# Second attention of a two-layer block: four score banks in turn, one bank and one exponential per head, values in two visits

## The chip, the cores and the metric

One core of a Trainium2 chip. The metric is the device time of one execution in microseconds (us). The engines are PE (TensorE, matmuls, with its weight loads apart as PEld), DVE (VectorE), ACT (ScalarE), POOL (GpSimd) and SP (SyncE, which issues DMAs). Each works through its own queue in order, and they meet at semaphores.

## The reference, cut to what matters

The kernel computes two layers on 4 x 512 tokens of width 256; each adds an attention and a mixture of experts to its input. The change lies in the attention of the second layer: 32 heads of dimension 8 in 8 groups, where the four heads of a group share keys and values.

```python
q = q.reshape(Bx, Sx, N_GROUPS, R, HEAD_DIM).transpose(0, 2, 3, 1, 4)
sim = jnp.einsum('bgrsd,bgtd->bgrst', q, k) / math.sqrt(HEAD_DIM)
attn = jax.nn.softmax(sim, axis=-1)
out = jnp.einsum('bgrst,bgtd->bgrsd', attn, v)
```

## The kernel before

The second attention works on one batch (512 tokens) and one group of heads at a time: 4 batches x 8 groups. A group has 16 pairs of a tile of 128 tokens (t, of 4) and a head (r, of 4). It is computed twice. First, `scores` (L814) makes the scores of 128 queries against 512 keys in one matmul (S0 to S15 below), and DVE's `reduce_max` (L1709) takes the maximum of each query. The maxima are negated and split into two parts (L1721, L1723), transposed by PE (`maxima_t`, L851; M below) and added to the stacked queries, into `qm` (L1702). Then `scores_t` (L820) computes the scores again, transposed (128 keys against 512 queries, T0 to T15 below) with the maxima already subtracted, ACT takes the exponential (L1206) into `pt`, and `values` (L830) multiplies with the values, one visit per tile of keys with four matmuls, one per head, in four column strips of the array. A ones column in the values gives the sums. For each two groups, ACT copies the result out of bank 7 (`outputs`, L1186), PE transposes it (`outputs_t`, L843) and DVE divides (`normalise`, L1671).

These steps are staged by hand. `stage(b, s)` stands in PE's, ACT's and DVE's programs with the same 16 steps i: PE issues S_i of group s, and beside them the later parts of group s - 1 and s - 2. `TRANSPOSED` (L860) gives the step at which each T is issued and `VALUED` (L861) that of each values visit; a step of 16 or more falls into the next stage. Before, T's go in eight pairs of heads into two double banks (3 and 4, 5 and 6), with one exponential of 1024 columns for each pair (T0 and T1 at step 4, and so on). Values tiles 0 and 1 are visited at step 15, tile 2 at step 3 of the next stage, tile 3 at its step 9. T0 waits for `qm` (L887). `turns` (L295) places the transposes of the maxima behind S2, those of the outputs (every second stage) behind step 11, and in three stages of a batch (s = 5, 6, 7) one third of the next batch's projection at step 13 (`project`, six matmuls, L547 to L549), and the transposes of its values (`values_by_key`, L807) at step 12 of the last. `compact` takes a projection out: first ACT (L1178 for queries; L1181 and L1183 for keys and values), then DVE the low part (L1661, L1664), at step 15 of DVE's stage.

S, M, the outputs, the projections and the values transposes share a ring of three banks: `next_bank` (L304) makes each use wait for the reader of the third use before it. `pt` has three tiles, so an exponential also waits for the values visit three tiles earlier (L1205). On SP, `stack_keys` (L367) loads the keys of four groups in turn and waits for the transposed scores of the group four back; `stack_queries` (L381) waits for `qm`. In the first batch DVE also does the routing of the second layer's experts, one small operation per step of a stage (`to_mask1`, `to_slots1`, L1694 and L1698; what is left of the second runs behind the batch's last stage, L1743).

Of the kernel before, what the change touches and what calls it, by code (L numbers as in the profile page):

```python
# [7 lines left out]
P = 128  # L8
# [4 lines left out]
QT = S // P  # L13
# [16 lines left out]
NG, R, HD = 8, 4, 8  # L30
# [11 lines left out]
def program(nc, x_in, aw0_in, aw1_in, ws0_in, moe0_in, moe1_in, pad_in, const_in, bias_in, out):  # L42
# [3 lines left out]
    with ctx:  # L46
# [83 lines left out]
        psum = ctx.enter_context(nc.psum_tensor("psum", [P, 8, 512], f32))  # L130
# [58 lines left out]
        km = [tr(R, S) for _ in range(4)]  # L189
        mz = tr(QT, P)  # L190
        qm_both = place("qm", on1 + 4104, [P, 2, S], f32r)
        qm = [qm_both[:, n, :] for n in range(2)]
        kv = tf(S)
        va = tf(QT, NG * 32)
        pt = [tf(R, S), tf(R, S), place("pt2", M + 32848, [P, R, S])]
# [56 lines left out]
        b_pj, b_kv, b_hi, b_lo, b_vt, b_va = (sem(n) for n in ("b_pj", "b_kv", "b_hi", "b_lo", "b_vt", "b_va"))  # L252
        b_qd, b_kd, b_sn, b_mx = (sem(n) for n in ("b_qd", "b_kd", "b_sn", "b_mx"))
        b_m1, b_m2, b_mt, b_qm, b_st, b_ex = (sem(n) for n in ("b_m1", "b_m2", "b_mt", "b_qm", "b_st", "b_ex"))
        b_km = sem("b_km")
        b_pv, b_ot, b_ox, b_rc, b_on, b_nt = (sem(n) for n in ("b_pv", "b_ot", "b_ox", "b_rc", "b_on", "b_nt"))
# [37 lines left out]

        def turns(s, following):  # L295
            never = QT * R
            return {"maxima": 2, "outputs": 11, "values": 12 if s == NG + 1 else never,
                    "project": 13 if following and NG - 3 <= s < NG else never}

        ring, read = {}, []

        def next_bank(engine, use, reader, value):  # L304
            if len(read) >= 3:
                engine.wait_ge(*read[-3])
            ring[use] = psum[:, (len(read) + 1) % 3, :]
            read.append((reader, value))
            return ring[use]

        @block.sync
        def _(sp):
# [9 lines left out]
            for l in range(2):  # L322
                n = ROWS[l] // PAD
# [43 lines left out]
            def stack_keys(u):  # L367
                b, g = u // NG, u % NG
                if g == 0:
                    sp.wait_ge(b_lo, 3 * b + (2 if b else 1))  # L370
                if u:
                    sp.wait_ge(b_kd, u * R * 16)
                if u < 4:
                    sp.wait_ge(b_km, u + 3)
                else:
                    sp.wait_ge(b_st, 2 * QT * (u - 3))
                for r in range(R):
                    sp.dma_start(km[u % 4][24 * r:24 * r + 24, r, :].bitcast(f32),
                                 kc[g * HD:(g + 1) * HD].bitcast(f32)).then_inc(b_kd, 16)
# [165 lines left out]
        def _(pe):  # L545
# [249 lines left out]
            routed(0, after_attention0)  # L795
            pe.wait_ge(m_y, pairs(0, NPAIR[0]))

            NP, NQ = NG * QT * R, NG * QT

            def project(n, b1, o):  # L800

# [17 lines left out]

            def scores_t(b, g, i):  # L820

                t, h = i // 2, i % 2
                if g >= 1 or i >= 2:
                    pe.wait_ge(b_ex, b * (2 * NQ) + (g * 2 * QT + i - 1))
                for r in (2 * h, 2 * h + 1):
                    ins = nc.tensor.matmul(psum[:, 3 + 2 * h + r % 2, :], km[g % 4][:, r, t * P:(t + 1) * P],  # L826
                                           qm[g % 2], start=True, stop=True)
                ins.then_inc(b_st, 1)

            def values(b, g, t):  # L830

                pe.wait_ge(b_ex, b * (2 * NQ) + ((g * QT + t) * 2 + 2))
                n = b * NG + g
                if t == 0 and g % 2 == 0 and n:
                    pe.wait_ge(b_ot, n // 2)
                if t == 0 and g % NG == 0:
                    pe.wait_ge(b_va, b + (g // NG + 1))
                for r in range(R):
                    ins = nc.tensor.matmul(psum[32 * r:32 * r + 32, 7, :], va[:, t, g % NG * 32:g % NG * 32 + 32], pt[(n * QT + t) % 3][:, r, :],  # L839
                                           start=(t == 0 and g % 2 == 0), stop=(t == QT - 1 and g % 2 == 1), tile_position=(0, 32 * r))  # L840
                ins.then_inc(b_pv, 1)
# [15 lines left out]

            TRANSPOSED = (4, 5, 8, 11, 12, 13, 16, 17)  # L860
            VALUED = (15, 15, 19, 25)  # L861

            def follow(b, g, step):
                for n in range(2 * QT):
                    if TRANSPOSED[n] == step:
                        scores_t(b, g, n)
                for t in range(QT):
                    if VALUED[t] == step:
                        values(b, g, t)
# [127 lines left out]
        def _(act):  # L997
# [161 lines left out]
            for b in range(B):  # L1159
                for k in (2, 3):  # L1160
                    r = k * T + b * S
# [6 lines left out]
            def compact(n, b1, o, at):  # L1168

                act.wait_ge(b_pj, b1 * 3 + (at + 1))  # L1170
                if not (isinstance(b1, int) and b1 == 0):
                    if n < 2:
                        act.wait_ge(b_qd, b1 * (NG * 16) - (1 - n) * (NG // 2) * 16)
                    else:
                        act.wait_ge(b_kd, b1 * (NG * R * 16))
                if n < 2:
                    for i in range(2):
                        ins = nc.scalar.activation(qc[:, n, i, :], o, ACT.Identity, bias=bq1[:, n:n + 1])  # L1178
                    ins.then_inc(b_hi, 1)
                else:  # L1180
                    nc.scalar.activation(kv[:], o, ACT.Identity, bias=bq1[:, 2:3]).then_inc(b_kv, 1)  # L1181
                    for i in (0, 2):
                        ins = nc.scalar.activation(kc[:, i, :], o, ACT.Identity, bias=bq1[:, 2:3])  # L1183
                    ins.then_inc(b_hi, 1)
# [8 lines left out]
            def stage(b, s, last):  # L1193
                back, following = s >= 1, not last and s >= 1
                for t in range(QT):
                    if isinstance(b, int) and (b, s, t) == (0, 2, 1):
                        gating_exp(E1, 2, TT)
                    if back:
                        g = s - 1
                        for h in range(2):  # L1200
                            if s >= 2 and s % 2 and (t, h) == (1, 1):
                                outputs(b, s - 2)
                            act.wait_ge(b_st, b * (2 * NG * QT) + ((g * QT + t) * 2 + h + 1))
                            if b * (NG * QT) + g * QT + t >= 3:
                                act.wait_ge(b_pv, b * (NG * QT) + (g * QT + t - 2))  # L1205
                            nc.scalar.activation(pt[((b * NG + g) * QT + t) % 3][:, 2 * h:2 * h + 2, :], psum[:, 3 + 2 * h:5 + 2 * h, :],  # L1206
                                                 ACT.Exp, scale=float(HD) ** -0.5).then_inc(b_ex, 1)
                    if t == 2 and following and NG - 3 <= s < NG:
                        compact((0, 2, 1)[s - (NG - 3)], b + 1, ring["projection", b * 3 + s - (NG - 3) + 4], s - (NG - 3))
                if last and s == NG:  # L1210
                    outputs(b, s - 1)

# [34 lines left out]
            for n in range(2 * B):  # L1247
                act.wait_ge(b_nt, n + 1)
                b, k = n // KH, n % KH
# [627 lines left out]
```

## Time and profile before

| | us |
|---|---|
| median of 3 runs (1142.21 to 1143.25) | 1142.29 |
| the profiled execution's own time | 1137.68 |
| its span, first to last instruction | 1135.9 |
| PE busy | 1009.3 |
| DVE busy | 758.9 |
| ACT busy | 592.8 |

The profile is of one execution, which was faster than the three timed ones; its rows add up to its own span. Busy times of PE are of pipelined matmuls with modelled ends. In rows of the chain of waits a number is the time that a piece added to the chain; in rows of the timeline it is the time from the start of the first to the end of the last instruction of a merged group, so overlaps are inside. An answer names tiles by the first tensor at their place: `work_f` and `pt` are the tiles of exponentials, `work_r` holds keys, queries and the negated maxima.

### The profile page before, as it was taken

The page shows a single profiled execution, that of the slowest core. Times are in us where ns is not written, and L with a number is a line of the kernel's source. Part 1 is how long each engine was busy: PE and PEld are TensorE (multiplying, and loading weights), DVE is VectorE, ACT ScalarE, POOL GpSimd, SP SyncE. Part 2 cuts the span into 40 slices and gives each one's busy share as a digit, 9 for nine tenths or more (in the row PEclk, how much of TensorE's full clock was granted, in tenths as well). Part 3 has the DMA queues.
Part 4 walks back from the last instruction along what each step waited for, and adds up shares of the span by engine and source line. Part 5 has one row for each costly group of instructions (what it writes and reads, how often), then busy time and mean ns, then how long its engine had stood idle before and what let it go on. Part 6 is the DMA issues. An engine that isn't in the chain of part 4 may idle for free.

```text
span 1135.9 us, 17330 instructions
## 1 busy us (share of the span) xinstructions
PE 1009.3 (89%) x5716; PEld 738.8 (65%) x5716; DVE 758.9 (67%) x1575; ACT 592.8 (52%) x895; POOL 318.2 (28%) x331
## 2 busy tenths in 40 slices
PE   4999995769999846799999999999999987999995
PEld 3877874669999814555554555555555565888884
DVE  6577553466665446799888888888888846444437
ACT  6325553265565543365655666566555655444431
POOL 2005777065654510000000122222221000455442
PEclk9999998789999958899999999999999998999999
DMA  6863333364434272011111222222222124333253
GB/s 223 326 270 116 127 107 118 104 198 144 135 127 135 95 310 36 12 30 29 29 29 29 43 55 58 56 56 56 56 57 43 63 72 156 108 107 101 91 198 137
DMA packets 49139, 120.48 MB, mean 106 GB/s; under 512 B 7752, under 2 KB 24904, under 8 KB 48520
## 3 DMA queue, kind: packets, MB, share of 16 engines
q1 hardware_dynamic: 36096, 82.80, 25.2%
q0 software_dynamic: 11808, 32.37, 7.5%
q10 hardware_dynamic: 1152, 4.19, 0.9%
q8 instruction: 52, 0.85, 0.3%
q14 instruction: 31, 0.25, 0.1%
HBM read 72.30 MB, written 52.42 MB: 110 GB/s over the span
## 4 chain that ended last, share of the span: by engine, by line
PE 65%; DVE 15%; POOL 7%; ACT 5%; issue 4%; DMA 3%; SPq 0%; ACTq 0%; DVEq 0%; POOLq 0%
PE psum L817 10%; PE psum L839 10%; PE psum L826 8%; POOL xg L466 5%; PE psum L633 5%; PE psum L634 4%; PE psum L635 4%; DVE work_f L1709 4%; PE psum L547 3%; PE psum L549 3%; PE psum L548 3%; PE psum L619 3%; PE psum L644 2%; ACT work_f L1206 1%; PE psum L665 1%
## 5 line engine op out<-in xcount | busy, mean ns | idle before, releaser
L1709 DVE TENSOR_REDUCE work_f<-psum 128x1 f32<-128x512 f32 x512 | 335.0, 685 | 51.2 <-PE psum L817 49.8
L1206 ACT ACTIVATE work_f<-psum 128x1024 f32<-128x1024 f32 x172 | 169.0, 1023 | 112.0 <-PE psum L826 110.4
L817 PE MATMUL psum<-work_r 128*128 128x512 f32 x512 | 205.2, 440 | 19.5 <-DVE work_f L1709 6.5
L473 POOL DMA_INDIRECT yk<-yb,dest x134 | 131.4, 980 | 238.7 <-ACT yb L1059 215.0
L817 PEld LDWEIGHTS psum<-work_r 128*128 128x128 f32 x512 | 94.2, 190 | 131.3 <-DVE work_f L1709 75.5
L826 PE MATMUL psum<-qm,work_r 128*128 128x512 f32 x512 | 161.9, 398 | 4.2 <-ACT work_f L1206 2.7
L466 POOL DMA_INDIRECT xg<-xn,slot x112 | 108.4, 968 | 180.5 <-PE psum L855 142.8
L826 PEld LDWEIGHTS psum<-qm,work_r 128*128 128x128 f32 x512 | 93.6, 188 | 31.8 <-ACT work_f L1206 10.9
L1206 ACT ACTIVATE pt<-psum 128x1024 f32<-128x1024 f32 x84 | 82.9, 1023 | 50.2 <-PE psum L826 49.3
L633 PE MATMUL psum<-wexp,xbh 128*128 x268 | 102.5, 382 | 6.9 <-issue 6.8
L634 PE MATMUL psum<-wexp,xbh 128*128 x268 | 96.6, 360 | 0.0
L635 PE MATMUL psum<-wexp,xbl 128*128 x268 | 96.1, 359 | 0.0
L839 PE MATMUL psum<-work_f 128*32 128x512 f32 x688 | 89.1, 601 | 0.6 <-ACT work_f L1206 0.6
L1044 ACT ACTIVATE sgb<-psum 128x352 f32<-128x352 f32 (+1 forms) x67 | 34.8, 519 | 98.2 <-PE psum L635 98.2
L1482 DVE TENSOR_TENSOR xbl<-psum,xbh 128x512 fp32r<-128x512 f32 x67 | 46.3, 691 | 58.0 <-ACT xbh L999 57.6
L1059 ACT ACTIVATE yb<-psum,share 128x256 f32<-128x256 f32 x134 | 56.3, 472 | 47.8 <-PE psum L661 24.5
L462 POOL TENSOR_TENSOR xn<-const 128x16 f32<-128x16 f32 x7 | 1.5, 220 | 259.0 <-PE psum L855 185.9
L1492 DVE TENSOR_TENSOR hb<-sgb,psum 128x352 f32<-128x352 f32 (+1 forms) x67 | 39.2, 584 | 51.0 <-ACT sgb L1044 50.8
L633 PEld LDWEIGHTS psum<-wexp,xbh 128*128 128x128 f32 x268 | 52.1, 194 | 13.5 <-issue 9.7
L619 PE MATMUL psum<-const,xb 128*128 128x128 f32 x268 | 42.2, 282 | 15.3 <-DVE xbl L1482 10.1
L635 PEld LDWEIGHTS psum<-wexp,xbl 128*128 128x128 f32 x268 | 52.3, 195 | 5.0
L634 PEld LDWEIGHTS psum<-wexp,xbh 128*128 128x128 f32 x268 | 52.2, 195 | 3.8
(218 smaller groups left out, 2034.9 us busy)
## 6 DMA issues: line engine op xcount, KB each, us to landing
xb<-xg SPq DMA_DIRECT2D x67, 258.0 KB
xg<-in_pad SPq DMA_DIRECT2D x1, 10320.0 KB
yg<-yk SPq DMA_DIRECT2D x20, 512.0 KB, 9.4
stage<-in_moe SPq DMA_DIRECT2D x16, 608.0 KB, 4.8
xg<-in_pad SPq DMA_DIRECT2D x1, 7224.0 KB
work_r<-work_r SPq DMA_DIRECT2D x128, 48.0 KB
work_r<-work_r SPq DMA_DIRECT2D x32, 192.0 KB
stage<-in_moe SPq DMA_DIRECT2D x16, 384.0 KB, 3.8
```

The costliest lines, as they stand in the source:

```text
L466: nc.gpsimd.indirect_dma_start(xg[l], bass.IndirectOffsetOnAxis(ap=slot[l][:, at:at + 1], axis=0), xn[l][:, t, :], None).then_inc(m_scat, 16)
L473: nc.gpsimd.indirect_dma_start(yk[l], bass.IndirectOffsetOnAxis(ap=dest[:, j % 8, i:i + 1], axis=0), yb[l][:, j % 2, i, :], None).then_inc ...
L619: ins = nc.tensor.transpose(psum[:, 4, (i * KH + c) * P:(i * KH + c + 1) * P], xb[l][:, j % 2, i, c * P:(c + 1) * P], ident)
L633: nc.tensor.matmul(o, xbh[l][:, j % 2, i * KH + c, :], hi, start=c == 0, stop=False)
L634: nc.tensor.matmul(o, xbh[l][:, j % 2, i * KH + c, :], lo, start=False, stop=False)
L635: ins = nc.tensor.matmul(o, xbl[l][:, j % 2, i * KH + c, :], hi, start=False, stop=c == KH - 1)
L817: nc.tensor.matmul(next_bank(pe, ("scores", n), b_mx, n + 1), qs[g % 2][:, t * P:(t + 1) * P], km[g % 4][:, r, :], start=True, stop=True). ...
L826: ins = nc.tensor.matmul(psum[:, 3 + 2 * h + r % 2, :], km[g % 4][:, r, t * P:(t + 1) * P], qm[g % 2], start=True, stop=True)
L839: ins = nc.tensor.matmul(psum[32 * r:32 * r + 32, 7, :], va[:, t, g % NG * 32:g % NG * 32 + 32], pt[(n * QT + t) % 3][:, r, :], start=(t = ...
L1059: ins = nc.scalar.activation(yb[l][:, j % 2, i, :], psum[:, 6, i * H:(i + 1) * H], ACT.Identity, scale=share[:, j % 8, i:i + 1])
L1206: nc.scalar.activation(pt[((b * NG + g) * QT + t) % 3][:, 2 * h:2 * h + 2, :], psum[:, 3 + 2 * h:5 + 2 * h, :], ACT.Exp, scale=float(HD) * ...
L1709: v.reduce_max(mx[:, s % 2, i:i + 1], ring["scores", n], AX.X).then_inc(b_mx, 1)
```

## The change

PE, ACT and DVE do the same arithmetic on the same data in another arrangement.

- The ring has four banks (0 to 3) from the seventeenth use on; each use waits for the reader of the fourth use before it.
- T's go one by one, at steps 4 to 19, into three single banks (4, 5, 6) in turn. T number m waits for the exponential of number m - 3, and ACT does one exponential of 512 columns for each.
- Values tiles 0 and 1 are visited at step 14 (behind S14 and T10), tiles 2 and 3 at step 22, which is step 6 of the next stage (between S6 and T2).
- The outputs are transposed at step 12, projections and values transposes at step 10. ACT takes a projection out ahead of exponential 7, DVE at its step 12.
- `stack_keys` counts 16 matmuls per group instead of 8 pairs.

```diff
-            return {"maxima": 2, "outputs": 11, "values": 12 if s == NG + 1 else never,
-                    "project": 13 if following and NG - 3 <= s < NG else never}
+            return {"maxima": 2, "outputs": 12, "values": 10 if s == NG + 1 else never,
+                    "project": 10 if following and NG - 3 <= s < NG else never}
...
-        ring, read = {}, []
+        ring, holder, uses = {}, {3: (b_va, 1)}, []
 
         def next_bank(engine, use, reader, value):
-            if len(read) >= 3:
-                engine.wait_ge(*read[-3])
-            ring[use] = psum[:, (len(read) + 1) % 3, :]
-            read.append((reader, value))
+            n = len(uses)
+            bank = (n + 1) % 3 if n < QT * R else (3, 2, 0, 1)[n % 4]
+            if bank in holder:
+                engine.wait_ge(*holder[bank])
+            ring[use] = psum[:, bank, :]
+            holder[bank] = (reader, value)
+            uses.append(bank)
             return ring[use]
+
+        def transposed_bank(m):
+            return psum[:, 4 + m % 3, :]
...
-                    sp.wait_ge(b_st, 2 * QT * (u - 3))
+                    sp.wait_ge(b_st, QT * R * (u - 3))
...
-                t, h = i // 2, i % 2
-                if g >= 1 or i >= 2:
-                    pe.wait_ge(b_ex, b * (2 * NQ) + (g * 2 * QT + i - 1))
-                for r in (2 * h, 2 * h + 1):
-                    ins = nc.tensor.matmul(psum[:, 3 + 2 * h + r % 2, :], km[g % 4][:, r, t * P:(t + 1) * P],
-                                           qm[g % 2], start=True, stop=True)
-                ins.then_inc(b_st, 1)
+                t, r = i // R, i % R
+                m = b * NP + g * QT * R + i
+                if m >= 3:
+                    pe.wait_ge(b_ex, m - 2)
+                nc.tensor.matmul(transposed_bank(m), km[g % 4][:, r, t * P:(t + 1) * P],
+                                 qm[g % 2], start=True, stop=True).then_inc(b_st, 1)
...
-                pe.wait_ge(b_ex, b * (2 * NQ) + ((g * QT + t) * 2 + 2))
+                pe.wait_ge(b_ex, b * NP + (g * QT + t + 1) * R)
...
-            TRANSPOSED = (4, 5, 8, 11, 12, 13, 16, 17)
-            VALUED = (15, 15, 19, 25)
+            TRANSPOSED = range(4, 4 + QT * R)
+            VALUED = (14, 14, 22, 22)
...
-                        g = s - 1
-                        for h in range(2):
-                            if s >= 2 and s % 2 and (t, h) == (1, 1):
+                        tile = (b * NG + s - 1) * QT + t
+                        for r in range(R):
+                            if s >= 2 and s % 2 and (t, r) == (1, 1):
                                 outputs(b, s - 2)
-                            act.wait_ge(b_st, b * (2 * NG * QT) + ((g * QT + t) * 2 + h + 1))
-                            if b * (NG * QT) + g * QT + t >= 3:
-                                act.wait_ge(b_pv, b * (NG * QT) + (g * QT + t - 2))
-                            nc.scalar.activation(pt[((b * NG + g) * QT + t) % 3][:, 2 * h:2 * h + 2, :], psum[:, 3 + 2 * h:5 + 2 * h, :],
+                            if (t, r) == (1, 3) and following and NG - 3 <= s < NG:
+                                compact((0, 2, 1)[s - (NG - 3)], b + 1, ring["projection", b * 3 + s - (NG - 3) + 4], s - (NG - 3))
+                            act.wait_ge(b_st, tile * R + r + 1)
+                            if tile >= 3:
+                                act.wait_ge(b_pv, tile - 2)
+                            nc.scalar.activation(pt[tile % 3][:, r, :], transposed_bank(tile * R + r),
                                                  ACT.Exp, scale=float(HD) ** -0.5).then_inc(b_ex, 1)
-                    if t == 2 and following and NG - 3 <= s < NG:
-                        compact((0, 2, 1)[s - (NG - 3)], b + 1, ring["projection", b * 3 + s - (NG - 3) + 4], s - (NG - 3))
```

## Rows read from the trace of the kernel before

**Rows 1.** The page's first part: busy us, share of the span, instructions.

```profile
span 1135.9 us, 17330 instructions
PE 1009.3 (89%) x5716; PEld 738.8 (65%) x5716; DVE 758.9 (67%) x1575; ACT 592.8 (52%) x895; POOL 318.2 (28%) x331
```

**Rows 2.** Busy time by stretch: batches, tail, an even, an odd, a last stage.

```profile
core 0: us, PE busy (x) PEld busy (x) DVE busy (x) ACT busy (x) POOL busy (x), PEclk, DMA share, GB/s
484.79:613.37 128.58, 123.05 (x658) 67.14 (x662) 115.05 (x269) 77.25 (x85) 0.00 (x0) 1.00 0.18 29
613.37:725.26 111.89, 108.44 (x586) 59.78 (x590) 95.26 (x169) 69.42 (x76) 18.20 (x22) 1.00 0.24 50
...
837.12:903.51 66.39, 64.84 (x356) 35.01 (x360) 58.83 (x105) 41.37 (x44) 5.77 (x6) 1.00 0.23 57
903.51:919.55 16.04, 14.18 (x90) 5.25 (x90) 2.14 (x5) 9.76 (x11) 0.00 (x0) 1.00 0.00 0
738.79:751.68 12.89, 12.71 (x73) 6.83 (x76) 11.27 (x20) 7.32 (x9) 2.88 (x3) 1.00 0.27 61
725.26:738.79 13.53, 13.14 (x77) 7.13 (x80) 12.10 (x23) 8.91 (x10) 2.89 (x3) 1.00 0.28 60
...
697.46:712.38 14.92, 13.82 (x80) 7.70 (x84) 12.89 (x24) 9.16 (x10) 2.88 (x3) 1.00 0.25 54
```

**Rows 3.** The chain in an even stage: start us, us that it adds, what.

```profile
738.79 1.85 PE psum L839 x16
740.64 0.43 PE psum L817
741.07 0.46 PE psum L826 x2
...
742.46 0.44 PE psum L855 x4
...
743.14 0.99 PE psum L839 x8
...
749.41 1.03 ACT pt L1206
...
750.49 0.72 PE psum L826 x2
```

**Rows 4.** PE's timeline, end of an odd stage: idle time and releaser in brackets.

```profile
738.06 0.73 PE L817 MATMUL psum<-work_r 128*128 128x512 f32 x2 [0.39 <-DVE on L1680]
```

**Rows 5.** ACT's timeline: 512-column copies, 1024-column exponentials, 512 columns with bias.

```profile
196.72 2.03 ACT L999 CAST work_r<-psum 128x512 fp32r<-128x512 f32 x4
...
745.07 1.94 ACT L1206 ACTIVATE work_f<-psum 128x1024 f32<-128x1024 f32 x2 [1.55 <-PE psum L826]
...
766.14 1.27 ACT L1178 ACTIVATE work_r<-psum,bias 128x512 fp32r<-128x512 f32 x2 [0.81 <-PE psum L549]
```

**Rows 6.** DVE's timeline: four reductions, and a last one followed by the next stage's.

```profile
748.71 2.48 DVE L1709 TENSOR_REDUCE work_f<-psum 128x1 f32<-128x512 f32 x4 [0.23 <-PE psum L817]
...
768.11 0.68 DVE L1709 TENSOR_REDUCE work_f<-psum 128x1 f32<-128x512 f32 x1
...
769.13 1.88 DVE L1709 TENSOR_REDUCE work_f<-psum 128x1 f32<-128x512 f32 x3
770.92 0.68 DVE L1702 TENSOR_TENSOR qm<-psum,work_r 128x512 fp32r<-128x512 f32 x1
```

**Rows 7.** Taking out projections: the chain (keys and values), DVE's timeline (queries).

```profile
780.47 0.69 ACT work_f L1181
781.16 1.17 ACT work_r L1183 x2
...
782.35 0.70 DVE work_r L1664
...
767.44 0.75 DVE L1661 SCALAR_TENSOR_TENSOR work_r<-psum,bias,work_r 128x512 fp32r<-128x512 f32 x1 [0.37 <-ACT work_r L1178]
```

**Rows 8.** DVE's timeline, end of the first batch: what stands behind the last maxima.

```profile
600.80 0.18 DVE L1723 SCALAR_TENSOR_TENSOR work_r<-work_f,work_r 128x16 fp32r<-128x16 f32 x1
...
603.01 1.89 DVE L1709 TENSOR_REDUCE work_f<-psum 128x1 f32<-128x512 f32 x3
```

More of the change, by code:

```diff
@@ L796, in _ @@
             pe.wait_ge(m_y, pairs(0, NPAIR[0]))
-            NP, NQ = NG * QT * R, NG * QT
+            NP = NG * QT * R
             def project(n, b1, o):
@@ L856, in maxima_t @@
                 ins.then_inc(b_mt, 1)
-            TRANSPOSED = (4, 5, 8, 11, 12, 13, 16, 17)
-            VALUED = (15, 15, 19, 25)
+            TRANSPOSED = range(4, 4 + QT * R)
+            VALUED = (14, 14, 22, 22)
             def follow(b, g, step):
-                for n in range(2 * QT):
+                for n in range(QT * R):
                     if TRANSPOSED[n] == step:
```

## The prediction, made before the change was run

> **What bounds the kernel now.** The page comes first: of the span of 1135.9 us TensorE (PE) is busy for 89% [rows 1], so it is the engine to follow. Next come the stretches. The second attention runs from about 485 to 920 us, at full clock throughout, and I cut it where PE starts a pair of values tiles: one batch of eight stages takes 111.9 us, a plain stage without outputs ("even") 12.89, one with outputs ("odd") 13.53, and DVE and ACT are busy for 95 and 69 us of a batch, so neither is full [rows 2]. The chain of waits inside one even stage shows what PE's time is made of [rows 3]: one score matmul follows another in 0.23 us (two in 0.46), four transposes take 0.44, a pair of values tiles 1.85, a single one 0.99, and the first matmul after any values visit 0.43, which is 0.20 more. What is left is waiting. An even stage waits once for an exponential (the 1.03 us row); the two matmuls behind it take 0.72 where two take 0.46, so a matmul whose wait isn't over when its weights could be loaded costs 0.26 beside the wait. An odd stage waits for the normalisation (the row names its releaser), because three score banks go round too quickly [rows 4].
>
> The profiled execution took 1137.68 us, the three timed runs 1142.29 in the median: 4.6 more. I work in differences and add them to the median.
>
> **What the change takes away.** Values in two pairs cost 2 x (1.85 + 0.20) = 4.10 us of PE a stage, against 2.05 + 2 x 1.19 = 4.43: it saves 0.33. Without waits an even stage is 32 score matmuls (32 x 0.2315 = 7.41), 0.44 and the values: 12.28 before, 11.95 after. So the exponential's wait costs 12.89 - 12.28 = 0.6 and goes, since each head has its bank; that for the normalisation costs 13.53 - 12.28 - 0.44 = 0.8 and goes too, since with four banks the score matmul behind the outputs reuses the bank of a score. The gain in view is 12.89 - 11.95 = 0.94 in an even stage.
>
> **What it adds on ACT.** Sixteen exponentials of 512 columns take the place of eight of 1024. The trace has none of 512; its nearest rows are 512-column copies out of PSUM without a bias, four in 2.03 us, so one each 0.48 and 0.59 long, and operations with a bias tensor, two in 1.27, so 0.585 and 0.69 [rows 5]. These are the two ends. The exponential has no bias tensor, and two of 1024 in 1.94 with 1.03 for one [rows 3] fit the first end (0.91 for the second, less 0.43 for 512 columns), so I take 0.49 and 0.59; ACT then has 7.8 us of them in a stage of 13. The Trainium skill ("ScalarE: Activation LUTs", What ACT_TABLE_LOAD costs) gives 186 ns + 0.833 ns a column, overlapping by 93 ns: an estimate of 0.61 and 0.52, near the row's end; the margin of 0.16 us named below would be gone, up to 0.3 in each of some 12 plain even stages.
>
> **What it moves, and what is late next.** Call t = 0 the start of the first values visit. S, T, M are a score matmul, a transposed one and the transposes of the maxima. Before, that visit stood behind S15, so the last maxima were reduced during it, and a single values tile at step 3 kept PE busy until qm was ready. Now it stands at step 14, before S15, and the second visit at step 6, behind the wait for qm. PE after the visit: S15 until 2.28, then T11, S0, T12, S1, T13, S2 until 3.66, M until 4.10, T14, S3, T15, S4 until 5.02. DVE cannot begin the last reduction before 2.32. In the trace a late last reduction is followed by the first of the next stage 1.02 us later (the two small operations that write the negated maxima lie between), that by two more and the addition into qm 1.79 later, and the addition takes 0.68; back to back, reductions follow at 0.60 [rows 6]. So qm is ready at 2.32 + 1.02 + 1.79 + 0.68 = 5.81. T0, and all PE work behind it, waits from 5.02 to 5.85 and pays 0.26: 1.1 us in every stage, more than the 0.94 above. The rest: T0 until 6.35, S5, T1, S6, second visit 7.04 to 8.89, T2 until 9.32, sixteen matmuls 3.70: next visit at 13.0. DVE's reductions and the exponentials keep up (the seventh exponential, for T10, ends at 12.38, and T10's weights could load at 12.54: margin 0.16). **Even stage 13.0**, against 12.89.
>
> An **odd** stage adds 0.44 of outputs. ACT's copy of the outputs (0.59) stands before exponential 5, which then ends at 11.9, while T8 could load at 11.6: 0.3. So 13.75, against 13.53; bounded by 13.45 and, at the slow end of the exponential, 14.2.
>
> **Projection stages**, three a batch for three batches. The projection moves from step 13 to 10. Its bank is held until ACT has copied it and DVE has subtracted. In the trace that takes 0.69 + 1.17 + 0.70 with small gaps, 2.6 us, for keys and values, and 1.27 + 0.75, 2.1 us, for queries [rows 7]. At step 13 the next matmul that needed the bank lay behind a 1.85 us values visit. Now it is the fourth use on: S14 in an even stage, six matmuls (1.39) later, S13 in an odd one, four matmuls and the outputs' transposes (1.37) later. PE waits 1.2 + 0.3 for keys and 0.75 + 0.3 for queries. The two query stages come to 13.0 + 0.44 + 1.39 + 1.05 = 15.85, the key stage to 13.0 + 1.39 + 1.5 = 15.9. The values transposes (step 10, last stage of a batch) only hold a short DVE copy: 13.0 + 0.44 + 0.44 = 13.9, and 1.0 less than its row, the only stage that clearly gains.
>
> One batch: 3 x 13.0 + 13.75 + 2 x 15.85 + 15.9 + 13.9 = 114.25, **+2.4** against 111.9, for the second and third batch. The first has the same plus DVE's routing steps: 2.1 us of them stand behind the last maxima [rows 8] and now lie wholly in front of qm: +4.5. The last has five plain stages before its tail, 3 x 13.75 + 2 x 13.0 = 67.25 against 66.39: +0.9. Its tail took 16.04; with all exponentials paced by ACT, the first visit behind T10 and two tiles left for the end instead of one, the walk gives T10 until 11.55, the visit until 13.4, the last exponential at 16.4 and two tiles: 18.5, **+2.5**.
>
> Costing nothing: SP's stacking of keys waits for the same sixteen matmuls of a group, two steps later, a whole stage before they are needed; queries wait for qm as before; POOL's scatters wait for none of the moved steps. If that cover were gone, PE would stand at step 0.
>
> Sum: 2 x 2.4 + 4.5 + 0.9 + 2.5 = 12.7 us: 1142.3 + 12.7 = 1155.0 (1150.4 for a profiled execution).
>
> **The rivals.**
> Faster: PE is kept full and the wait for qm isn't there. For it speaks that all three engines have room [rows 2] and that the waits of today go. Its point is the stretch from a visit to T0: it wins only if S15's maxima are done by the visit's end, as they were. Then a batch is 102.0 us, the last five stages 61.1: 3 x 9.9 + 5.3 = 35 less, 1107. Against it: S15 is issued behind the visit on PE's own queue. The Trainium skill ("Perfetto Trace Analysis", Optimizing Scalar/DVE Operations) says that where ScalarE or VectorE isn't saturated but makes bubbles on other engines, breaking up instructions may finish work sooner; that is this case by the trace, where ACT is busy for 69 of 112 us, and speaks for this rival. 8%.
> No change: the wait for qm comes, but the projections' bank and T8 don't wait. A batch is then 110.4, -1.5; the sum is -3.0 + 0.6 + 0 + 2.5, 1142.4. Against it: the latencies are rows, not guesses. 12%.
> Slower still: the exponential costs the biased end. Exponential 7 would end at 12.97, T10 pay 0.5 in twelve even stages and 0.4 in six odd ones: +8.5, 1163.5. 20%.
> The forecast keeps 60%, with its own range of 1149 to 1160.
>
> **How the numbers follow.** The range of 1142 to 1166 takes in the forecast, the slow exponential and half of the no-change case; outside lie the faster rival and the ends, under 2 in 10. A measurement of this kernel can tell 0.2%, 2.3 us, from no change. Faster: the first rival and a little of the second, 0.10. Same: the rest of the second, 0.09. Slower: 0.81.
>
> **What would show it.** Right: in the stage after each visit, a PE wait of about 0.8 us for the addition into qm, some 30 times; waits of a score matmul for the low part of a projection, nine times, 0.7 to 1.3 us; the exponentials near 0.59 us, no normalisation waits, no exponential waits in even stages; stages of 13.0 and 13.75. Wrong: no PE wait for qm (then the first rival), or exponentials of 0.69, or T's waiting for them in every stage.

## The result, and the profile after

| us | before | after |
|---|---|---|
| median of 4 runs each, in turn on one chip | 1142.77 (1142.21 to 1143.52) | 1156.55 (1154.57 to 1157.09) |
| ratio of the two, with its 95% interval | | 1.012 [1.0104, 1.0136] |
| the profiled execution's own time | 1137.68 | 1157.02 |
| its span | 1135.9 | 1155.2 |
| attention stretch: first values visit to the end of the last | 434.76 | 450.68 |

The change makes the kernel 13.8 us slower between the medians; 12.7 had been predicted, 1155.0 in all. The stretch in the third line is where the change lies, and most of its plain stages repeat to a few hundredths of a us (single ones take longer, by 0.4 in these two kernels), so most of what follows is read there. It grew by 15.9 us. The two spans differ by 19.3: 3.9 of that lies ahead of the stretch, where the profile of before was the faster by 5.4 us already at the last sum of the first layer (it begins at 414.39 before and at 419.80 after, in code that the change does not touch), and -0.5 behind it.

The page of the changed kernel, its first part and one of the costliest groups (out<-in, partitions x elements, count, then busy us, mean ns of one, idle time before it):

```profile
PE 1010.1 (87%) x5716; PEld 746.2 (65%) x5716; DVE 750.1 (65%) x1575; ACT 608.2 (53%) x1151; POOL 317.8 (28%) x331
...
L1213 ACT ACTIVATE work_f<-psum 128x512 f32<-128x512 f32 x344 | 185.2, 612 | 112.1 <-PE psum L832 111.9
```

Against [rows 1], PE does the same 5716 matmuls in the same busy time (1010.1 against 1009.3), in a span 19 us longer; what came is idle time. ACT has 256 instructions and 15 us more, and still is busy for 53% only. An exponential of 512 columns lasts 0.612 us.

The stretches of the changed kernel, which answer to [rows 2] (first batch, second batch, last five plain stages, tail; then an even stage, an odd one, the last stage of a batch, one with a query projection and the one with keys and values):

```profile
488.66:622.91 134.25, 121.24 (x658) 67.54 (x662) 113.76 (x269) 81.59 (x157) 0.00 (x0) 1.00 0.18 28
622.91:738.46 115.55, 106.88 (x586) 60.66 (x590) 91.69 (x169) 72.92 (x140) 18.15 (x22) 1.00 0.23 49
854.05:921.78 67.73, 63.92 (x357) 35.72 (x360) 55.82 (x104) 43.29 (x84) 5.75 (x6) 1.00 0.22 56
921.78:939.34 17.56, 16.29 (x92) 5.71 (x92) 3.12 (x9) 11.45 (x23) 0.00 (x0) 1.00 0.00 0
752.32:765.38 13.06, 12.37 (x73) 6.95 (x76) 10.65 (x22) 8.07 (x17) 2.87 (x3) 1.00 0.25 60
738.46:752.32 13.86, 13.07 (x76) 7.27 (x80) 11.50 (x22) 9.05 (x18) 2.88 (x3) 1.00 0.27 59
711.13:725.40 14.27, 13.49 (x80) 7.74 (x84) 11.92 (x23) 9.04 (x18) 2.87 (x3) 1.00 0.25 57
765.38:781.30 15.92, 14.44 (x83) 8.48 (x86) 12.44 (x23) 10.30 (x20) 2.88 (x3) 1.00 0.22 51
781.30:797.30 16.00, 14.02 (x79) 8.00 (x82) 11.87 (x24) 10.27 (x20) 2.88 (x3) 1.00 0.13 38
```

The clock is at 1.00 in all of them. PE is busy for 12.37 of an even stage's 13.06 us where it had 12.71 of 12.89: the saving of PE's work came (0.34 by these rows), and 0.69 us of idle time came with it. The chain of waits in that even stage shows where it comes from, and answers to [rows 3]:

```profile
752.32 1.85 PE psum L844 x16
754.17 0.45 PE psum L823
...
754.64 0.70 DVE work_f L1714
...
755.37 0.19 DVE work_r L1726
...
755.76 1.80 DVE work_f L1714 x3
757.55 0.61 DVE qm L1707
...
758.21 0.50 PE psum L832
...
759.39 1.85 PE psum L844 x16
```

Read it downwards: the visit, S15 behind it, and then the chain leaves PE. DVE reduces S15, writes the negated maxima, reduces three more, adds into `qm`; only then T0. PE's own timeline names the wait in brackets, and the list of waits over the whole attention counts it (engine and line, releaser: us in total, times, longest):

```profile
758.21 0.50 PE L832 MATMUL psum<-qm,work_r 128*128 128x512 f32 x1 [0.69 <-DVE qm L1707]
```

```profile
PE psum L832 <- DVE qm L1707: 23.0, 32, 1.1
...
PE psum L823 <- DVE work_r L1666: 4.7, 6, 0.8
PE psum L823 <- DVE work_r L1669: 3.8, 3, 1.3
```

One wait for `qm` in each of the 32 groups, where the kernel before had none on PE; six for a query projection's low part, three for that of keys and values. The waits for the normalisation [rows 4], 15 of 5.0 and 2.4 us in all before, are gone, as are the even stages' for an exponential.

### The profile page after: what moved, and what is told of

The parts are those of the page before. It is cut to its first block, busy times and chain, and to the rows that moved or that the text cites. A ratio compares the mean times of both kernels' runs of the same rounds, so it can differ in the third digit from the quotient of the medians.

```text
span 1155.2 us, 17836 instructions
## 1 busy us (share of the span) xinstructions
PE 1010.1 (87%) x5716; PEld 746.2 (65%) x5716; DVE 750.1 (65%) x1575; ACT 608.2 (53%) x1151; POOL 317.8 (28%) x331
## 4 chain that ended last, share of the span: by engine, by line
PE 59%; DVE 20%; POOL 7%; issue 5%; ACT 4%; DMA 3%; SPq 0%; ACTq 0%; DVEq 0%; POOLq 0%
PE psum L844 10%; DVE work_f L1714 8%; PE psum L832 7%; PE psum L823 6%; POOL xg L472 5%; PE psum L639 5%; PE psum L640 4%; PE psum L641 4%; PE psum L553 3%; PE psum L555 3%; PE psum L554 3%; PE psum L625 3%; PE psum L650 2%; DVE qm L1707 2%; PE psum L671 1%
## 5 line engine op out<-in xcount | busy, mean ns | idle before, releaser
L1714 DVE TENSOR_REDUCE work_f<-psum 128x1 f32<-128x512 f32 x512 | 324.7, 681 | 77.9 <-PE psum L823 76.2
L1213 ACT ACTIVATE work_f<-psum 128x512 f32<-128x512 f32 x344 | 185.2, 612 | 112.1 <-PE psum L832 111.9
L823 PE MATMUL psum<-work_r 128*128 128x512 f32 x512 | 213.5, 420 | 22.6 <-DVE work_f L1714 8.2
L832 PE MATMUL psum<-qm,work_r 128*128 128x512 f32 x512 | 211.9, 417 | 24.1 <-DVE qm L1707 23.0
L823 PEld LDWEIGHTS psum<-work_r 128*128 128x128 f32 x512 | 97.2, 191 | 80.9 <-DVE work_f L1714 46.5
L1213 ACT ACTIVATE pt<-psum 128x512 f32<-128x512 f32 x168 | 92.8, 612 | 56.9 <-PE psum L832 54.8
L844 PE MATMUL psum<-work_f 128*32 128x512 f32 x688 | 86.7, 598 | 0.0
```

The lines of the kernel that those rows point to most:

```text
L823: nc.tensor.matmul(next_bank(pe, ("scores", n), b_mx, n + 1), qs[g % 2][:, t * P:(t + 1) * P], km[g % 4][:, r, :], start=True, stop=True). ...
L832: nc.tensor.matmul(transposed_bank(m), km[g % 4][:, r, t * P:(t + 1) * P], qm[g % 2], start=True, stop=True).then_inc(b_st, 1)
L1213: nc.scalar.activation(pt[tile % 3][:, r, :], transposed_bank(tile * R + r), ACT.Exp, scale=float(HD) ** -0.5).then_inc(b_ex, 1)
L1714: v.reduce_max(mx[:, s % 2, i:i + 1], ring["scores", n], AX.X).then_inc(b_mx, 1)
```

## The experiments

Each is the changed kernel with a few numbers edited, or, once, the kernel before. "Stretch" is the attention stretch of its profiled execution; ratios are to the kernel before on the same chip. All stretches but those of before, after and "banks and heads alone" hold a few us at a lower clock in the first batch, told of at the end; the even and odd stages are free of it.

| run | median us | ratio, 95% | stretch | even | odd |
|---|---|---|---|---|---|
| before | | | 434.76 | 12.89 | 13.53 |
| after | 1156.55 | 1.012 [1.0104, 1.0136] | 450.68 | 13.06 | 13.86 |
| first visit at 15 | 1141.87 | 0.9996 [0.9974, 1.0018] | 435.98 | 12.50 | 13.3 |
| second visit at 19 | 1128.73 | 0.9898 [0.9864, 0.9933] | 424.55 | 12.22 | 12.88 |
| projections at 12 | 1149.28 | 1.0079 [1.0051, 1.0108] | 444.78 | 13.06 | 13.86 |
| maxima behind S3 | 1181.91 | 1.0355 [1.0317, 1.0392] | 473.01 | 13.67 | 14.44 |
| visits at 15 and 19 | 1132.08 | 0.9897 [0.985, 0.9944] | 425.45 | 12.31 | 12.91 |
| banks and heads alone | 1130.56 | 0.9885 [0.9841, 0.993] | 422.36 | 12.24 | 13.39 |
| visits alone | 1189.8 | 1.0394 [1.0349, 1.044] | 480.46 | 14.3 | 15.08 |
| outputs' copy earlier | 1157.38, one run | | 450.9 | 13.06 | 13.50 |
| 19, projections, copy | 1127.24 | 0.9851 [0.9809, 0.9894] | 416.10 | 12.23 | 12.83 |
| the same again | 1120.95 | 0.9803 [0.9776, 0.983] | 416.58 | 12.22 | 12.83 |
| the same, first visit at 13 | 1133.9 | 0.9909 [0.9887, 0.9931] | 426.52 | 12.23 | 12.83 |

### Where the wait comes from: the visits and the maxima moved

The theory: S15 stands behind the first visit on PE's queue, so the last maxima come late, and nothing long enough lies between them and T0. Rivals: the second visit's place, the projections' bank, the exponentials. The first run puts the visit back behind S15.

```diff
-            VALUED = (14, 14, 22, 22)
+            VALUED = (15, 15, 22, 22)
```

> The changed kernel with one edit: the first values visit stands one step later, behind S15 (and T11), the second stays at step 6. Theory (order of the queue): the last maxima are then reduced during the visit, so qm is ready before PE comes to T0; the wait of 1.1 us goes in each of some 31 stages: 1156.5 - 34 = about 1122, an even stage of 12.0 instead of 13.06, and no PE wait for the addition into qm. Rival (heads): what was lost is lost to sixteen single transposed scores with sixteen small exponentials in place of eight pairs; the place of the visit doesn't matter: 1156 plus or minus 3, and the wait comes back under another name.

The stage came down by 0.56 and the stretch by 14.7, to about that of before, but it was to come down twice as far: a miss by half. The chain in this run says why:

```profile
752.64 1.85 PE psum L844 x16
754.50 0.44 PE psum L823
...
754.96 1.89 DVE work_f L1714 x3
756.85 0.61 DVE qm L1707
...
757.50 0.50 PE psum L832
```

S15's maxima now are done during the visit, but S0 to S2 of the next group stand behind it, DVE takes S0 to S2 first, and the addition into `qm` is behind them in DVE's queue. It is DVE's own order, three reductions and the addition, that is left: 3.0 us from the visit's end to T0, against 2.7 us of PE work (in the prediction's walk it was 3.2; S15 and T11 now go ahead of the visit). The list of waits has 12.0 us in 32 waits instead of 23.0: most shrank from 0.69 to about 0.29, and the 0.26 of a matmul whose weights could not be loaded early is paid in full.

The second run leaves the first visit at 14 and puts the second one between the late maxima and T0.

```diff
-            VALUED = (14, 14, 22, 22)
+            VALUED = (14, 14, 19, 19)
```

> The changed kernel with the first visit left at step 14 and the second moved from step 22 to step 19 (step 3 of the next stage, ahead of T0). Theory (order of the queue): the chain to qm is as late as in the changed kernel, but PE has 2.05 us of values to do ahead of T0 instead of behind it, which covers the 0.8 us; about 1122 again, by the other end of the same wait. Rival (heads): 1156 plus or minus 3. A second rival (the last reduction must not be late, whatever covers it): 1156 here and 1122 for the first kernel.

That takes the wait away. In the list of waits of this run `qm` is left once (for the first group, at 480.40, ahead of the first values visit), and in an even stage's chain the second visit stands where the wait had been, with DVE's part off the chain:

```profile
PE psum L832 <- DVE qm L1707: 0.7, 1, 0.7
```

```profile
734.84 1.85 PE psum L844 x16
736.69 0.43 PE psum L823
...
738.50 0.48 PE psum L860 x4
...
739.68 1.85 PE psum L844 x16
```

The even stage is 12.22, not the 11.95 that PE's work adds up to: S13 and S14, the last two ahead of the first visit, take 0.34 and 0.36 instead of 0.23, their weight loads having waited 0.21 and 0.30 for reductions, and the maxima's transposes 0.48. The stretch fell by 26.1. Changing one number of the place of two tiles turns the change from 1.2% slower to 1.0% faster; so the order, not the work, made it slower. With both visits moved, at 15 and 19, it is the same to 1 us of the stretch:

> Both moves of the visits at once: the first at step 15 (behind S15), the second at step 19 (ahead of T0). Theory: qm is ready 1.0 us earlier after the first visit than with step 14, but with step 19 the wait is covered already, so nothing more is to be had there: within 0.3% of the second kernel, 1126 to 1131. If the wait for qm still cost something there, it would be faster than that.

The opposite was tried too: the transposes of the maxima one step later make `qm` later still.

```diff
-            return {"maxima": 2, "outputs": 12, "values": 10 if s == NG + 1 else never,
+            return {"maxima": 3, "outputs": 12, "values": 10 if s == NG + 1 else never,
```

> The changed kernel with the transposes of the maxima one step later (behind S3 instead of S2), so that DVE adds into qm behind four reductions instead of three. The suspected wait is made longer by one reduction. Theory: 0.6 us more in each of some 32 stages, 1156.5 + 19 = about 1175, and the PE wait for qm grows from 0.7 to 1.3 us in every stage. Rival (heads, or any cause beside the chain to qm): 1156 plus or minus 3, since PE's own work is the same.

Each plain stage grew by 0.6, the time from one reduction to the next, and PE's waits for `qm` from 23.0 us to 40.0. Nothing hides any of it: `qm` sets the stage. The whole grew by more than the 19 us expected, to 1181.91; in the profiled execution two stages of the first batch also hold the lower clock told of at the end.

### The projections' bank

```diff
-                    "project": 10 if following and NG - 3 <= s < NG else never}
+                    "project": 12 if following and NG - 3 <= s < NG else never}
...
-                            if (t, r) == (1, 3) and following and NG - 3 <= s < NG:
+                            if (t, r) == (2, 1) and following and NG - 3 <= s < NG:
...
-                    if i == turn["project"] + 2:
+                    if i == turn["project"] + 3:
```

> The changed kernel with the projection at step 12 instead of 10, ACT taking it out ahead of exponential 9 instead of 7, DVE at its step 15 instead of 12. The values visits stay where the change put them. Theory: the fourth use of the ring behind the projection is then S0, behind a values visit, and the bank's wait is covered; the three projection stages of a batch fall from 16.28, 15.99 and 15.95 to 14.9, 14.5 and 14.9, 4.0 less a batch for three batches: 1156.5 - 12 = about 1144.5. Rival (the projection costs its six matmuls and its copies wherever it stands): 1156 plus or minus 2.

In the third batch the three stages went from 15.92, 16.00 and 15.94 to 15.26, 14.46 and 15.26, and no matmul waits for a projection's low part any more: the bank was the cause. Nine such stages save 8.6 us, less than expected, because a wait beside it stayed. In the chain of a stage with queries of this run, T8 waits for the exponential that stands behind ACT's copy of the outputs:

```profile
769.41 0.43 ACT work_f L1004
...
769.88 0.65 ACT work_f L1213
...
770.57 0.50 PE psum L832
```

And the stretch shows 5.9 us, not 8.6, as one stage of the first batch took 2.7 longer than in the changed kernel (18.14 against 15.45). TensorE's clock is lower in it; that is taken up at the end. The copy was then moved alone, in the changed kernel, three exponentials ahead; a plain odd stage of that run, in the view of the stretches above, follows the text on record.

```diff
-                            if s >= 2 and s % 2 and (t, r) == (1, 1):
+                            if s >= 2 and s % 2 and (t, r) == (0, 2):
```

> The changed kernel with one edit on ACT: the copy of the outputs stands ahead of exponential 2 instead of exponential 5, in the 1.9 us in which ACT waits for T2. Theory: plain odd stages fall by the 0.3 us that T8 waited, from 13.86 to 13.5, even stages stay at 13.06. Rival (the odd stage's excess is the outputs' transposes or the normalisation): 13.86 stays. About 2 to 3 us in the whole, too little for one look to tell, so the stages decide.

```profile
736.97:750.47 13.50, 12.80 (x77) 7.19 (x80) 11.13 (x21) 9.03 (x18) 2.88 (x3) 1.00 0.27 60
```

Odd stages lost 0.36, to 13.50 against an even 13.06 and 0.44 of outputs: the T8 wait is gone. The last stage of a batch stayed at 14.28, so its excess has another cause. The stretch did not show the gain, for in this execution too that stage of the first batch was longer (16.78), and one of the second batch (16.87 against 16.28, not followed).

### Which part of the change costs: heads or visits

Banks and heads as changed, with visits, outputs, values and projections at their places of before:

```diff
-            VALUED = (14, 14, 22, 22)
+            VALUED = (15, 15, 19, 25)
...
-            return {"maxima": 2, "outputs": 12, "values": 10 if s == NG + 1 else never,
-                    "project": 10 if following and NG - 3 <= s < NG else never}
+            return {"maxima": 2, "outputs": 11, "values": 12 if s == NG + 1 else never,
+                    "project": 13 if following and NG - 3 <= s < NG else never}
...
-                            if (t, r) == (1, 3) and following and NG - 3 <= s < NG:
+                            if (t, r) == (3, 0) and following and NG - 3 <= s < NG:
```

> The changed kernel's banks and heads (four banks in turn, three single banks, an exponential per head) with everything else where the kernel before has it: values visits at 15, 15, 19 and 25, outputs at 11, values transposes at 12, the projection at 13 and taken out at the end. Theory (the loss is the moved visits and projections, the banks and heads are a gain): the waits for the exponential (0.6) and the normalisation (0.8) go, 3 x 0.6 + 5 x 0.8 = 5.8 less in a batch of 111.9, up to 25 us: 1117 to 1125. Rival (heads: sixteen small exponentials and single banks are the loss): 1150 or more.

This part by itself gains 1.15%: 12.4 us of the stretch. That is the forecast direction, but less than the 17 to 25 us expected, as one wait stayed. An even stage takes 12.24, against 12.28 for PE's work without waits. So the exponential per head and its banks are no cost in this arrangement, and the rival that they are the loss has fallen. The odd stage keeps its wait for the normalisation, seen in PE's timeline of this run; it also counts as it did before (9 waits of a score matmul, 4.8 us, against 9 of 5.0):

```profile
731.81 0.50 PE L823 MATMUL psum<-work_r 128*128 128x512 f32 x1 [0.42 <-DVE on L1685]
```

So four banks by themselves do not take the normalisation's wait away; the prediction's reason was not enough. ACT's copy of the outputs (until 728.87) and their transposes (at 729.40) are on time in this run; DVE's normalisation stands behind reductions in its queue and ends at 731.75, and S15, the fourth use of the ring behind the outputs, is due before the first visit. In the changed kernel and in every run without this wait the outputs stand at step 12 instead of 11, so that the fourth use is S0, behind the visit. I read the cause so from the queues; no run moved the outputs alone.

The visits alone, in the kernel before (the moved projections, outputs and values transposes are in neither of these two runs):

```diff
-            VALUED = (15, 15, 19, 25)
+            VALUED = (14, 14, 22, 22)
```

> The kernel before with one edit: values visits at 14, 14, 22 and 22, its three score banks, pairs of heads and projections left as they are. Theory: the wait for qm comes here too; PE has 2.9 us of work between the visit's end and T0 against 4.0 us of DVE's chain, so 1.1 + 0.26 a stage, less the 0.33 of the merged visits and some of the 0.6 of the exponential's wait: 0.4 to 1.0 us a stage more, 1155 to 1173. Rival (the moved visits are a gain by themselves, 0.33 a stage): 1132.

It costs 3.9%, 45.6 us, more than I had expected, and the two parts don't add up to the whole: -13.6 and +45.6 make +32, the whole change, which has the moved projections besides, +13.8. The chain of an odd stage of this run (15.08 us) holds the wait for `qm` once more, and others behind it:

```profile
757.81 1.85 PE psum L839 x16
...
761.25 1.79 DVE work_f L1709 x3
763.04 0.61 DVE qm L1702
...
765.36 1.85 PE psum L839 x16
...
767.69 1.30 DVE work_f L1709 x2
...
769.03 0.50 PE psum L817
```

Behind the first visit the chain runs over DVE to `qm`, as in the changed kernel; behind the second it runs over two more reductions before PE has a bank again. In the changed kernel nothing of the second kind is on the chain of an even or odd stage; I put that down to the fourth bank, and no run changed the banks alone. The score matmuls' waits for the normalisation are still there too, nine of 5.1 us in all, though the last tile is visited at step 6. So heads and banks paid for part of what the visits cost. How the 45.6 us divide between these waits wasn't measured.

### Putting it together

The second visit at 19, projections at 12 as above, and the copy of the outputs ahead of the first exponential of the stage:

```diff
-            VALUED = (14, 14, 22, 22)
+            VALUED = (14, 14, 19, 19)
...
-                            if s >= 2 and s % 2 and (t, r) == (1, 1):
+                            if s >= 2 and s % 2 and (t, r) == (0, 0):
```

> The second kernel's values schedule (14, 14, 19, 19) with the other two waits taken away as well: the projection at step 12 and taken out later, as in the third kernel, and ACT's copy of the outputs ahead of exponential 0 instead of exponential 5, where ACT is idle for 1.9 us. Theory (three waits, each with its own place): from the second kernel's 107.8 us a batch, the three projection stages (14.9, 14.9, 14.8) fall by 1.1, 1.5 and 1.1, in three batches, and the odd stages by up to 0.3: 1128.7 - 11 - 2 = about 1116, ratio 0.977. Rival (the projection's wait was already covered once the visits were moved): 1127.

> The fifth kernel once more, beside the one above on the same chip, with more rounds: ratio to the kernel before 0.981 to 0.989, as in its first run, and batches of 104.9 us.

Run twice, on two chips, it took 416.10 and 416.58 us of the stretch, 18 less than the kernel before and 34 less than the changed one, with ratios of 0.9851 and 0.9803: the best version here. The gain is smaller than expected (0.977). The projection stages fell, but by 0.8, 1.4 and 0.7 us (from 14.86, 14.90 and 14.84 to 14.09, 13.48 and 14.16) instead of 1.1, 1.5 and 1.1, and the odd stages by 0.05 instead of 0.3. The first run's median, 1127.24, is by itself the rival's 1127; but the second kernel's list still has nine waits for a projection's low part, 8.5 us, and this one's has none. Its third batch, and in it a stage with queries and the one with keys and values, in the second of these runs:

```profile
717.20:822.07 104.87, 104.66 (x586) 60.28 (x590) 91.38 (x169) 72.58 (x140) 23.49 (x26) 1.00 0.27 62
742.25:756.34 14.09, 14.09 (x83) 8.46 (x86) 11.78 (x22) 9.33 (x19) 2.88 (x3) 1.00 0.26 59
756.34:769.82 13.48, 13.48 (x79) 8.03 (x82) 12.21 (x25) 9.42 (x19) 2.88 (x3) 1.00 0.15 45
```

PE is busy for 104.66 of 104.87 us, so waits as long as those above are nowhere left in it. A batch is 7.0 us shorter than before, and 10.7 shorter than in the changed kernel.

One more place for the first visit, ahead of S14:

```diff
-            VALUED = (14, 14, 19, 19)
+            VALUED = (13, 13, 19, 19)
```

> The fifth kernel (all three waits covered, visits at 14 and 19) with the first visit one step earlier still, at 13, so that the two visits stand further apart (6 and 10 steps instead of 5 and 11) and DVE runs dry less. The theory says that an early first visit is harmless as long as the second one covers the wait for qm: even stages between 11.95 and 12.24, so 0 to 2 us less a batch, ratio to the kernel before 0.977 to 0.986. If the lateness of the last maxima cost something of its own, it would be slower than the fifth kernel.

A miss. Even stages stay at 12.23 and the projection stages grow (13.48 to 14.53 for keys, the queries from 14.09 and 14.16 to 14.22 and 15.06), and an even stage behind them from 12.23 to 13.14, which wasn't followed. With two score matmuls behind the visit, DVE's part of the projection stands behind a reduction that is fed only after it, and a score matmul waits for that in the chain:

```profile
765.90 0.49 DVE work_f L1714
...
766.51 0.75 DVE work_r L1666
...
767.40 0.47 PE psum L823
```

## Why the prediction was right, step by step

| step | predicted | measured |
|---|---|---|
| even stage | 13.0 | 13.06 |
| odd stage | 13.75 | 13.86 |
| stages with queries | 15.85 | 15.92, 15.94 |
| stage with keys and values | 15.9 | 16.00 |
| last stage of a batch | 13.9 | 14.27 |
| a batch against before | +2.4 | +3.7 |
| first batch | +4.5 | +5.7 |
| last five plain stages | +0.9 | +1.3 |
| tail | +2.5 (18.5) | +1.5 (17.56) |
| attention in all | +12.7 | +15.9 |

**The wait for `qm`**, on which the sign rests, came as walked through: `qm` ready 5.81 us after the visit's start, measured 5.84 (758.16 less 752.32); PE is idle for 0.69 there by its timeline, and the stage is 1.1 us longer than PE's work without waits (13.06 against 11.95), more than the 0.94 that the edit saves. The runs show it as the cause, not only as a row: with the second visit as cover it is gone and the stage is 0.84 shorter; with later maxima it grows by as much as these are late.

**The projections' bank** came too, in nine stages, with waits of 0.8 for queries and 1.3 for keys; moving the projection takes them away. T8's wait behind the outputs' copy was predicted at 0.3, and moving the copy gave 0.36. The normalisation's wait went as predicted, but not by the four banks alone, as the run with banks and heads shows.

**The exponential.** Alone it takes 0.612 where I took 0.59, and four in a row take 2.08 by ACT's timeline:

```profile
762.68 2.08 ACT L1213 ACTIVATE pt<-psum 128x512 f32<-128x512 f32 x4
```

That is (2.08 - 0.61) / 3 = 0.49 apart, as taken from the copies; the price with a bias was the wrong neighbour, and the rival built on it is out. The Trainium skill ("ScalarE: Activation LUTs", What ACT_TABLE_LOAD costs) had led to an estimate of 0.61 for one and 0.52 apart: the trace agrees with the first and is 0.03 under the second, and that 0.03 is what would have cost the margin of 0.16.

**What was mis-sized.** The last stage of a batch: the prediction said that the values transposes "only hold a short DVE copy". Short it is, but it stands in DVE's queue behind five reductions, and its bank with it. In the chain of that stage of the changed kernel S13 waits for it:

```profile
720.74 3.08 DVE work_f L1714 x5
723.82 0.34 DVE work_f L1673
...
724.21 0.50 PE psum L823
```

That is 0.37 a batch. The other stages each came out 0.06 to 0.11 longer than the walk, which over a batch's seven makes 0.55, and a single stage now and then took 0.4 more (16.28 for 15.92 in the second batch); with these the 1.3 us by which a batch is over is accounted for. (The query stage's own terms add up to 15.88, not 15.85.)

The first batch is over by the same 1.2, but that its 2.1 us of routing fit is partly luck. The stage in which the routing stands ahead of `qm` grew by 1.2 (14.28 to 15.45), not by 2.1 beside a plain even stage's 0.2: before, PE already waited there, which the prediction left out. In its timeline:

```profile
603.85 0.63 PE L855 MATMUL psum<-const,work_r 128*128 128x128 f32 x4 [1.09 <-DVE work_f L1709]
```

Most of the rest came in three earlier stages, where small steps of the routing stand between DVE's reductions and PE's waits for `qm` are 0.90 to 0.99 instead of 0.69.

In the tail I put both last tiles behind the last exponential. It ends at 16.45 as predicted (16.4), but tile 2 needs only T11's and is multiplied before that: one tile, 0.94, less. By these the attention's sum was 3.2 us low; the medians differ by 13.8, closer to the forecast, but that is luck: a difference of 2 us between the two is within what the untouched stretches vary.

**The rivals.** The faster one had a sound core. The rule in the Trainium skill ("Perfetto Trace Analysis", Optimizing Scalar/DVE Operations), that breaking up instructions can finish work sooner where an engine isn't full but makes others wait, agrees with the run with banks and heads alone (0.9885; the even stage lost its wait for the exponential, 12.89 to 12.24), though that run changed the banks as well. That rival's condition, S15's maxima done by the visit's end, wasn't even enough: the first experiment fulfils it and only draws level, with an even stage of 12.50 against 11.95. It needed cover between `qm` and T0.

## What to carry to other kernels

Where one engine's queue holds work of a dependent chain and long independent pieces, the place of a long piece decides whether it is cover or delay: put it between the moment when the other engine begins its chain and the first instruction that needs the result, and look at what stands behind it on both queues. Count a bank's time from the matmul to its reader's end, queue of the reader included, and not by the reader's own length. A change with a gain and a loss in it should be split and its parts run alone: here the heads and banks were a gain by themselves and the visits a loss, and moving one pair of tiles by three steps turned 1.2% slower into 1.0% faster.

## What the runs showed of the hardware that I had not expected

It concerns the clock of TensorE in one stage of the first batch. In that stage DVE's routing stands ahead of `qm`, and PE waits twice, 1.83 us for a reduction and 0.60 to 0.70 for `qm`, with some matmuls between. In the changed kernel the granted clock stayed at 1.00 after it; in the run with the projections at 12, at the end of the same waits, it fell to 0.50 (1.2 GHz) and stayed there for the 5.65 us that follow; the visit in them took 3.57 us instead of 1.85. First the stretches of the changed kernel (the waits, then what follows), then those of that run:

```profile
607.46:615.72 8.26, 5.66 (x33) 2.65 (x32) 7.95 (x21) 3.43 (x7) 0.00 (x0) 1.00 0.00 0
615.72:620.35 4.63, 4.63 (x27) 2.48 (x28) 3.21 (x6) 2.20 (x5) 0.00 (x0) 1.00 0.44 75
```

```profile
600.70:608.95 8.25, 5.75 (x32) 2.64 (x31) 7.94 (x21) 3.43 (x7) 0.00 (x0) 0.94 0.00 0
608.95:614.60 5.65, 5.65 (x21) 1.83 (x21) 2.52 (x4) 1.19 (x2) 0.00 (x0) 0.50 0.45 72
```

The granted clock fell at the end of the first batch in ten of the eleven profiled experiments (not with banks and heads alone; twice with the maxima behind S3), and neither in the profile of before nor in that of the changed kernel; elsewhere in the attention it stayed at 1.00. In the run where it can be compared it cost 2.7 us. So the lower clock followed waits of the same length in one execution and not in the other (the projections ahead of them stand two steps later in the second run, so the work is not quite the same). Whether the executions without a profile had it isn't known, and no run took the waits there away.

Whole executions of the kernel before took between 1137.68 and 1149.8 us, while most plain stages repeat to 0.05 us. The one kernel that was profiled twice took 1128.17 and 1123.75 us in all, and 416.10 and 416.58 in the stretch, so there most of what varies lies outside the stretch studied here; for the ratio of two arrangements the stages say more than the totals.
